# The last two batches of a cross-attention kernel: scores of two units issued one behind the other, products and projections between the pairs

## The reference

```python
Q = (query @ Wq.T + bq).reshape(B, Sq, N_HEADS, D_K).transpose(0, 2, 1, 3)
K = (key_value @ Wk.T + bk).reshape(B, Skv, N_HEADS, D_K).transpose(0, 2, 1, 3)
V = (key_value @ Wv.T + bv).reshape(B, Skv, N_HEADS, D_K).transpose(0, 2, 1, 3)
scores = jnp.einsum('bhqd,bhkd->bhqk', Q, K) / np.sqrt(D_K)
attn = jax.nn.softmax(scores, axis=-1)
context = jnp.einsum('bhqk,bhkd->bhqd', attn, V).transpose(0, 2, 1, 3).reshape(B, Sq, D_MODEL)
x = context @ W_o.T + b_o + query
mu = jnp.mean(x, axis=-1, keepdims=True)
var = jnp.mean(jnp.square(x - mu), axis=-1, keepdims=True)
return (x - mu) / jnp.sqrt(var + LN_EPS) * ln_gamma + ln_beta
```

## Time and profile before

| | us |
|---|---|
| median of 3 executions | 149.48 (149.32 to 150.67) |
| the profiled execution's own time | 148.18 |
| its span, first to last instruction | 146.4 |
| TensorE busy in the span | 132.2 (90%) |
| VectorE, ScalarE, GpSimd busy | 94.6, 88.9, 82.4 |

### The profile page before, as it was taken

How to read it: one execution, slowest core, us unless ns; L and a number is a source line. 1 busy time by engine, 2 the same in 40 slices (tenths; PEclk the granted TensorE clock), 3 DMA queues, 4 the chain that set the end, 5 groups by cost and what they waited for, 6 DMA issues and landing times.

```text
span 146.4 us, 3925 instructions
## 1 busy us (share of the span) xinstructions
PE 132.2 (90%) x1479; PEld 116.1 (79%) x1479; DVE 94.6 (65%) x223; ACT 88.9 (61%) x180; POOL 82.4 (56%) x101
## 2 busy tenths in 40 slices
PE   5799999799999789698999999999999999999950
PEld 4599778589799668588898989898989888878620
DVE  3446798797857745467657776877687787521532
ACT  3637734648587826647586678665867566787410
POOL 8963998394429441300429998991247006597441
PEclk9999999999999999999999999999999999999996
DMA  4985895584039999670007104651071000011111
GB/s 117 352 312 180 241 343 174 196 250 173 4 83 226 283 238 252 216 239 23 8 0 262 56 6 129 197 204 29 24 263 53 16 26 4 4 36 34 36 31 31
DMA packets 15731, 19.59 MB, mean 134 GB/s; under 512 B 2544, under 2 KB 14896, under 8 KB 15712
## 3 DMA queue, kind: packets, MB, share of 16 engines
q1 hardware_dynamic: 14656, 17.36, 37.2%
q0 software_dynamic: 592, 1.70, 4.7%
q10 hardware_dynamic: 464, 0.28, 0.6%
HBM read 6.30 MB, written 0.92 MB: 49 GB/s over the span
## 4 chain that ended last, share of the span: by engine, by line
PE 65%; SPq 13%; DMA 12%; DVE 3%; issue 2%; ACT 2%; ACTq 1%; POOLq 0%; DVEq 0%
PE m_bank L860 15%; PE pv_bank L952 13%; PE st_bank L934 12%; PE mx_bank L901 11%; SPq L269 6%; SPq L321 5%; PE m_bank L983 4%; DMA q_stack<-shift 4%; DMA k_stack<-k_hl 3%; DMA c_raw<-ctxT 3%; PE m_bank L963 2%; PE mx_bank L934 2%; DMA q_stack<-q_hl 2%; DVE mx L717 1%; SPq L354 1%
## 5 line engine op out<-in xcount | busy, mean ns | idle before, releaser
L717 DVE TENSOR_REDUCE mx<-mx_bank 112x1 f32<-112x375 f32 x128 | 64.1, 541 | 24.5 <-PE mx_bank L901 24.2
L617 ACT ACTIVATE pw<-st_bank 125x448 f32<-125x448 f32 x86 | 45.5, 544 | 23.0 <-PE st_bank L934 22.6
L901 PE MATMUL mx_bank<-k_stack,q_stack 128*112 128x376 f32 x128 | 43.8, 354 | 3.2 <-DMA k_stack<-k_hl 1.7
L934 PE MATMUL st_bank<-q_stack,k_stack 128*125 128x224 f32 x172 | 35.0, 285 | 2.0 <-DMA q_stack<-shift 1.4
L934 PEld LDWEIGHTS st_bank<-q_stack,k_stack 128*125 128x125 f32 x172 | 28.6, 186 | 5.4 <-issue 2.0
L901 PEld LDWEIGHTS mx_bank<-k_stack,q_stack 128*112 128x112 f32 x128 | 22.2, 176 | 6.4 <-issue 1.9
L421 POOL TENSOR_TENSOR k_hl<-k_full,k_hl 128x376 fp32r<-128x376 f32 x10 | 10.0, 1005 | 21.6 <-ACT k_hl L538 21.6
L952 PE MATMUL pv_bank<-pw,v_sb 125*17 125x112 f32 x744 | 21.7, 260 | 0.0
L395 POOL TENSOR_TENSOR c_hl<-c_raw,c_hl 128x752 fp32r<-128x752 f32 x6 | 10.9, 1810 | 16.2 <-ACT c_hl L509 16.2
L860 PE MATMUL m_bank<-c_hl,w_hl 128*128 128x376 f32 x84 | 18.5, 362 | 1.1 <-ACT w_hl L501 0.8
L952 PEld LDWEIGHTS pv_bank<-pw,v_sb 125*17 125x17 f32 x744 | 16.6, 97 | 3.2 <-issue 1.9
(11 more groups left out here) (111 smaller groups left out, 171.5 us busy)
## 6 DMA issues: line engine op xcount, KB each, us to landing
k_stack<-k_hl SPq DMA_DIRECT2D x48, 188.0 KB, 2.5
c_raw<-ctxT SPq DMA_DIRECT2D x8, 375.0 KB, 4.1
q_stack<-q_hl SPq DMA_DIRECT2D x12, 112.0 KB, 2.3
q_stack<-q_hl SPq DMA_DIRECT2D x6, 168.0 KB, 3.4
x_space<-x_nat POOLq DMA_DIRECT2D x1, 896.0 KB, 11.0
out<-yo SPq DMA_DIRECT2D x8, 112.0 KB, 2.0
pw<-wT SPq DMA_DIRECT2D x2, 256.0 KB, 4.6
x_space<-xT SPq DMA_DIRECT2D x2, 224.0 KB, 5.5
```

The costliest lines, as they stand in the source:

```text
L617: nc.scalar.activation(p_tile[0:KC, n % PR, :, :], st_of(n)[0:KC, 0:4 * Q].rearrange("p (j q) -> p j q", j=4), ACT.Exp, scale=float(DK) ** ...
L717: nc.vector.tensor_reduce(mx[b % 2][:, h % 2, q_pair(h // 2):q_pair(h // 2) + 1], mx_bank[n % MR][0:Q, 0:KV], axis=AX_X, op=ALU.max, negat ...
L901: nc.tensor.matmul(mx_bank[n % MR][0:Q, 0:KVP], q_stack[k][:, side, q_pair(h // 2), b - Q_STACKS[k][0], :], k_stack[b % 3][:, h // 2, :], ...
L934: last = nc.tensor.matmul(st_of(n)[0:KC, k * 2 * Q:(k + 1) * 2 * Q], k_stack[i % 3][:, 2 * g + k, c * KC:(c + 1) * KC], q_stack[qk][:, :, ...
```

## The change

Three things change, all for units 76 to 95.

1. TensorE issues the scores of two units (u and u + 1, u even) one behind the other at the even unit, and none at the odd one. The products stand in a table, PV_AT, and come behind the pair that begins with units 76, 80, 82, 84, 88, 92 and 94.
2. The ring begins with the two `mx_bank`. Units 76 and 77 therefore wait for `max_read` at 128, and units 78 and 79 write `st_bank`.
3. ScalarE takes `o_raw` of batch 6 behind unit 1 of batch 7, no longer behind unit 2. The three small pieces at the end that wrote `st_bank` write `mx_bank`. `residual` and the first transposes of the last batch come at u = 10, behind units 94 and 95.

```diff
-S0_JOBS += [("ONT_HALF", 0), ("ONT_HALF", 1)]
-S1_JOBS.append(("OT_LAST", 1))
-JOBS = (M0_JOBS, M1_JOBS, S0_JOBS, S1_JOBS)
+X0_JOBS = [("ONT_HALF", 0), ("ONT_HALF", 1)]
+X1_JOBS = [("OT_LAST", 1)]
+JOBS = (M0_JOBS, M1_JOBS, S0_JOBS, S1_JOBS, X0_JOBS, X1_JOBS)
...
-        wide_ring = st_bank + mx_bank[0:2]
+        wide_ring = mx_bank[0:2] + st_bank
+        PV_AT = {WIDE: (B - 2, 0), WIDE + 4: (B - 2, 1), WIDE + 6: (B - 2, 2), WIDE + 8: (B - 2, 3),
+                 WIDE + 12: (B - 1, 0), WIDE + 16: (B - 1, 1), WIDE + 18: (B - 1, 2)}
...
-                    if u == (1 if i < B - 1 else 2) and i >= 1:
+                    if u == 1 and i >= 1:
                         take_o(i - 1)
...
-                if n < WIDE + 2:
+                if n < WIDE:
                     if n >= 2:
                         pe.wait_ge(exp_done, n - 1)
-                elif n < WIDE + len(wide_ring):
+                elif n < WIDE + 2:
                     pe.wait_ge(max_read, B * H)
                 else:
                     pe.wait_ge(exp_done, n - len(wide_ring) + 1)
...
-                    shifted_scores(i, u)
-                    if u == UNITS - 1 and i == B - 1:
+                    if n < WIDE:
+                        shifted_scores(i, u)
+                    elif u % 2 == 0:
+                        for v in (u, u + 1):
+                            shifted_scores(i, v)
+                    if u == UNITS - 2 and i == B - 1:
                         residual()
...
-                    if i == B - 1 and u in (5, 8, 11):
-                        values(i, u // NC - 1)
-                    elif n >= SINGLE and u % NC == 1 + (n > LATE) and not (i == B - 1 and u > 2):
-                        values(*divmod(n // NC - 1, NG))
-                    elif n < SINGLE and u % HALF == 1 and n > 2:
+                    if n >= WIDE:
+                        if n in PV_AT:
+                            values(*PV_AT[n])
+                    elif u % HALF == 1 and n > 2:
                         for group in (n // NC - 2, n // NC - 1):
                             values(*divmod(group, NG))
```

More of the change, by code:

```diff
@@ L160, in build @@
         pv_bank = bank("pv_bank")
-        m_bank = [bank(f"m_bank{i}") for i in range(2)] + st_bank
+        m_bank = [bank(f"m_bank{i}") for i in range(2)] + st_bank + mx_bank[0:2]
         bqk_in, bv_in, const_in, xb_in = sem("bqk_in"), sem("bv_in"), sem("const_in"), sem("xb_in")
@@ L198, in build @@
         WIDE = UNITS * (B - 2) + 4
-        LATE = WIDE + 2
-        SINGLE = UNITS * (B - 2) + NC
-        wide_ring = st_bank + mx_bank[0:2]
+        wide_ring = mx_bank[0:2] + st_bank
+        PV_AT = {WIDE: (B - 2, 0), WIDE + 4: (B - 2, 1), WIDE + 6: (B - 2, 2), WIDE + 8: (B - 2, 3),
+                 WIDE + 12: (B - 1, 0), WIDE + 16: (B - 1, 1), WIDE + 18: (B - 1, 2)}
         LAST = (slice(0, 2), slice(2, 3), slice(3, 4))
```

## The result

The changed kernel took 149.19 us (median of 20 executions, 147.99 to 152.23) beside 148.55 us for the kernel before (20 executions, 146.03 to 152.22). The ratio is 1.0112, with a 95% interval of 1.0062 to 1.0163: slower, by something between 0.6 and 1.6% on this measure. The ratio and its interval are taken only from the executions within 1.5% of the fastest one of each kernel; the medians of all twenty lie 0.64 us apart, 0.4%. So the times alone don't fix the size of the loss, and what follows rests on the traces. The forecast was 0.6% more, inside 1%.

A forecast was written before the change was run, and what follows sets the result against it. TensorE's order and waits were taken to bound the kernel. The terms 0.45 + 0.10 + 0.64 − 0.30 gave +0.9 us, on the median of 149.48 a forecast of 150.4 us, 0.6% more; range 149.1 to 151.3.

The forecast's parts named there:

- The bound: TensorE's order and waits set the end; a microsecond more there between 123 and 137 us adds one to the kernel.
- Nothing gained by pairs: Units 76 to 95: eleven runs of scores become eight, saving 0 us, since the 0.20 belongs to leaving a product.
- The wait that goes, −0.30: Batch 6's OT no longer waits for ScalarE's copy of `o_raw`, which comes earlier, with a product ahead of OT: −0.30 us.
- (a): Units 76 and 77, the first pair, wait for the last maximum on a drained array: +0.45 us, bounds 0.30 to 0.55.
- (b): Batch 7's transposed maxima, the shift's DMA and unit 84 all move later together: 0 us, with a bound of +0.15.
- (c): Exponentials: batch 7's group 0 product waits for unit 86's; batch 6's groups 2 and 3 don't wait: +0.10 us, bounds 0 and 0.2.
- (d): Batch 6's ONT waits for VectorE's 0.75 us behind OT, with two units as cover: +0.64 us, bounds 0.45 to 0.75.
- (e): VectorE and GpSimd: batch 5's statistics come about 1.5 us later, yet GpSimd finishes before the last batch needs it: 0 us.
- the bracket at its end: `residual` and the last transposes keep their places on the list, their banks having been read units earlier: 0 us.
- The covered waits: Rival: the last reduction is in time or VectorE hands over sooner, so only −0.30 stands: 148.6 to 149.5 us, chance 0.16.
- The clock: Rival: idling before ONT drops TensorE's clock to 1.2 GHz, doubling 3.2 us of work: 153.6 us, chance 0.04.
- The late exponentials: Rival: ScalarE 0.3 us late, products and unit 84 wait, another 0.6 to 0.8 us: 151.1 us, chance 0.18.

The follow-up runs named there:

- The product in front: Changed kernel with the product of batch 6's group 0 issued ahead of units 76 and 77: batch 3's projection to VectorE's last statistics 23.89 us, against 24.30.
- the products two by two: Changed kernel with batch 6's products issued two groups together, behind units 80/81 and 84/85: batch 3's projection to VectorE's last statistics 23.89 us, against 24.30.
- Moving one block: Changed kernel with batch 6's four transposes (OT) ahead of batch 7's group 0 product: batch 3's projection to VectorE's last statistics 23.64 us, against 24.30.
- the second profiles: Both kernels profiled again, unedited: batch 3's projection to VectorE's last statistics 24.30 us in the changed kernel, 23.33 us in the kernel before.

## Why the prediction was right, and where not

**The bound.** Right. The loss is on TensorE's chain, and the work of the other engines in T is the same to 0.02 us.

**Nothing gained by pairs.** Right. Fewer runs of scores brought nothing: a pair in flow is twice 0.21 to 0.22, the exit from a product costs 0.19 to 0.20 before scores and projection and 0.15 before OT, and the sum below closes without a term for pairs.

**The wait that goes, −0.30.** Nearly right in size. Before, OT and the unit behind the product took 0.12 + 0.62 + 0.41 = 1.15 us; now OT, which stands behind the product, takes 0.59 and a unit 0.22, together 0.81: −0.34. The share I gave to ScalarE's earlier copy was wrong. The experiment with the copy alone left T at 23.32, since the copy starts when the last product of batch 6 ends.

**(a), forecast +0.45.** From the start of T to the end of the transposed maxima it is 6.92 us before (118.57 to 125.49) and 7.33 in the changed kernel (121.36 to 128.69): +0.41. The pair started 0.05 behind VectorE's end, not 0.11. The product in front took all of it away (0.41).

**(b), forecast 0.** Right: from there to the end of the product of group 2 it is 2.90 us in both (125.49 to 128.39, 128.69 to 131.59). The slack that I put at 0.1 us is small: when the products two by two took work from this place, unit 84 came to wait, most likely for this DMA.

**(c), forecast +0.10.** The product took 0.75 instead of 0.70: +0.05.

**(d), forecast +0.64.** OT ends at 136.17 and ONT at 137.44, so 1.27 us, where I had 1.25; beside 0.61 to 0.63 without a wait, +0.65. Moving one block took it away.

**(e) and the bracket at its end, forecast 0.** The part on GpSimd is right: the chain does not pass through GpSimd anywhere in T. The step that failed is the bracket, "`residual` and the last transposes keep their places on the list". The residual's bank is `m_bank1`, and its last user is the projection of batch 6, which VectorE must first have summed (L750). Before, 0.64 us of scores (units 93 to 95) stood between that projection and the residual. Now there are two units, 0.43, beside VectorE's 0.43 and two handovers (0.02 and 0.05), and the residual's matmul overlaps nothing ahead of it (0.69 instead of 0.56): from the projection's end at 139.64 to the residual's at 140.84 is 1.20 us, where 0.43 + 0.56 = 0.99 would do, +0.21. Taking the residual to the tail gave 0.24 us more in the changed kernel than in the kernel before, which confirms it. It is the same mechanism as (d), at a third place, and I did not look for it there, although ONT's wait on z_ready, for the same bank, stands in the orders of the change.

**The sum.** 0.41 + 0.05 + 0.65 + 0.21 − 0.34 = 0.98 us, as measured in T, forecast 0.9. The missed 0.21 was partly made up by (a) and (c) being smaller and by the gain being larger; that the total came so close is in part luck. The experiments say the same: taken away one at a time, the three waits gave back 0.66 (with the 0.05 of (c)), 0.41 and 0.24, together 1.31 us, which is 0.98 and the 0.33 that the change had won.

**The time.** 0.98 us is 0.66% of 148.55, at the lower end of the interval of 0.62 to 1.63% and above the 0.4% between the medians. Whether the rest is chance or something outside T was not settled. The instructions ahead of T are the same in both kernels, and the second profiles reached T at 118.63 and 118.97, which speaks for chance. The forecast of 150.4 us stood on a median of three executions, 149.48, that twenty put at 148.55. So 149.19 lies at the very bottom of the stated 149.1 to 151.3 because of this base, and not because of the mechanism; about the mechanism, T says more than the time.

**The rivals.** The covered waits fell: both waits are in the timeline. The clock fell: the granted clock stayed at 1.00 through an idle of 0.47 us, and in T it was 1.00 in all twelve kernels. The late exponentials cost no more than the 0.05 us of (c) in the changed kernel, but they are close: eight units with only OT among them brought them (0.68 for 0.44).

## What to carry to other kernels

When blocks are regrouped on a busy engine, list for each block what it asks of another engine and how much work stands between the question and the answer; here three requests to VectorE lost their cover (for instance 0.75 us of its work against two units of 0.21), while the number of blocks and their prices stayed the same. Put the longest block between question and answer, look at banks that are used again as well as at data, and compare with the time at which the next instruction would *start* in flow, 0.25 us ahead of its predecessor's end here. And where times vary by more than the change, measure the stretch between two instructions: T repeated to 0.02 us where whole executions of one kernel lay up to 6 us apart.

## What the runs showed of the hardware

Two products together (48 matmul records of four column blocks) took 1.27 us and one took 0.70, so the second costs 0.57. By these figures about 0.13 us is paid once for each run of products, besides the 0.20 us at its exit; where in the run it falls, no trace here shows. I had put entering a product at nothing in the forecast, and its 0.70 held that share. And the residual, 0.43 us of matmul in an idle of about 0.4 us of the tail, cost 0.04 us: the idle there could be filled almost whole.
